# Attention in 256 steps: swaps issued by GpSimd, query pieces a step sooner, outputs ahead of the rests, high parts and value products a step later

## What is computed

```python
q = _rms_norm(x @ wq_a.T, q_norm_w) @ wq_b.T                 # 32 heads of 128 + 64
q_pe = _apply_rope(q_pe, cos, sin)                           # x1*cos - x2*sin, x1*sin + x2*cos
kv_c, k_pe = split(x @ wkv_a.T)                              # 64 latent, 64 rotated
k_nope, v = split(_rms_norm(kv_c, kv_norm_w) @ wkv_b.T)
scores = (q_nope . k_nope + q_pe . k_pe) * scale             # causal
out = softmax(scores) @ v
return out @ wo.T
```

## Time and profile before

| | us |
|---|---|
| median of 3 runs | 1619.09 |
| lowest, highest | 1617.4, 1630.4 |
| the profiled execution's time | 1624.83 |
| its span, first to last instruction | 1622.9 |
| long `least` of the first and of the last step start at | 259.5, 1380.0 |

### The profile page before, as it was taken

The page is one execution under the profiler, slowest core; times in us unless marked ns, Lnnn a source line. Parts: engine busy times, 40 slices in busy tenths (PEclk is TensorE's granted clock), DMA queues, the critical chain, the costliest instruction groups (busy, mean ns, idle before and its releaser), DMA issues. The chain is left out here.

```text
span 1622.9 us, 31480 instructions
## 1 busy us (share of the span) xinstructions
PE 1314.2 (81%) x12688; PEld 965.0 (59%) x12688; DVE 1058.3 (65%) x1441; ACT 940.8 (58%) x1466; POOL 660.6 (41%) x512
## 2 busy tenths in 40 slices
PE   4899976777788787777888777788877788599997
PEld 4678764555555555555555555555555555488886
DVE  3755527777777777777778777677877678422221
ACT  3554426766667676666767766676767677412111
POOL 0211104555555654455556545555655652000000
PEclk8999989999899999999999999999999999799998
DMA  4111035999998999999999999999999999733331
GB/s 148 42 36 52 26 105 110 171 183 181 175 190 171 193 172 183 184 185 187 185 189 185 184 183 186 189 180 187 181 187 187 185 187 185 200 116 119 137 131 65
DMA packets 673150, 253.36 MB, mean 156 GB/s; under 512 B 606336, under 2 KB 650112, under 8 KB 670080
## 3 DMA queue, kind: packets, MB, share of 16 engines
q1 hardware_dynamic: 670304, 242.68, 75.4%
q0 software_dynamic: 2720, 8.92, 1.7%
HBM read 58.60 MB, written 25.17 MB: 52 GB/s over the span
## 5 line engine op out<-in xcount | busy, mean ns | idle before, releaser
L816 DVE TENSOR_TENSOR prob_hl_sb<-prob_sb,prob_hl_sb 128x1152 f16<-128x1152 f32 x256 | 428.1, 1672 | 166.7 <-ACT prob_hl_sb L730 165.9
L667 PE MATMUL acc<-ch,prob_t_sb 128*128 128x65 f16 x2304 | 250.5, 199 | 204.1 <-DMA prob_t_sb<-prob_hl_sb 146.3
L667 PEld LDWEIGHTS acc<-ch,prob_t_sb 128*128 128x128 f16 x2304 | 217.2, 99 | 245.4 <-DMA prob_t_sb<-prob_hl_sb 120.6
L730 ACT ACTIVATE prob_hl_sb<-prob_sb 128x1152 f16<-128x1152 f32 x256 | 297.6, 1163 | 62.1 <-DMA prob_t_sb<-prob_hl_sb 60.8
L811 DVE TENSOR_REDUCE shift_sb<-score_long 128x1 f32<-128x1024 f32 (+3 forms) x256 | 260.5, 1018 | 92.9 <-PE score_long L653 92.9
L722 ACT ACTIVATE prob_sb<-score_long,shift_sb 128x1024 f32<-128x1024 f32 (+3 forms) x256 | 243.2, 950 | 101.6 <-DVE shift_sb L811 99.7
L794 POOL TENSOR_TENSOR rot_sb<-rot_sb,sinT_sb 128x512 f32<-128x512 f32 x62 | 97.8, 1577 | 382.7 <-DMA rot_sb<-qf_sb 382.7
L668 PE MATMUL acc<-cl,prob_t_sb 128*128 128x64 f16 x2304 | 249.8, 196 | 0.0
L669 PE MATMUL acc<-ch,prob_t_sb 128*128 128x65 f16 x2304 | 249.0, 197 | 0.0
L669 PEld LDWEIGHTS acc<-ch,prob_t_sb 128*128 128x128 f16 x2304 | 219.7, 100 | 0.0
L668 PEld LDWEIGHTS acc<-cl,prob_t_sb 128*128 128x128 f16 x2304 | 219.3, 101 | 0.0
(11 more groups left out here) (161 smaller groups left out, 2659.6 us busy)
## 6 DMA issues: line engine op xcount, KB each, us to landing
o_nat_sb<-o SPq DMA_DIRECT2D x18, 1024.0 KB, 5.1
rot_sb<-qf_sb SPq DMA_DIRECT2D x256, 64.0 KB, 2.1
o<-o_sb SPq DMA_DIRECT2D x32, 512.0 KB, 3.9
wqk_sb<-wqk SPq DMA_DIRECT2D x32, 320.0 KB, 3.3
wo_sb<-wo SPq DMA_DIRECT2D x16, 512.0 KB, 4.3
y_in_sb<-y POOLq DMA_DIRECT2D x18, 256.0 KB, 3.0
x_sb<-x SPq DMA_DIRECT2D x4, 1024.0 KB, 4.9
y<-y_sb SPq DMA_DIRECT2D x16, 256.0 KB, 2.0
```

Of the source, the lines that this page charges most:

```text
L667: nc.tensor.matmul(acc[:, at:at + KVL + 1], hi, high, start=(j == 0), stop=False)
L730: nc.scalar.activation(prob_hl[:, s % NHL, 0, :], prob[:, s % 2, :], ACT.Copy).then_inc(hi_ready, 1)
L816: nc.vector.tensor_tensor(prob_hl[:, s % NHL, 1, :], prob[:, s % 2, :], prob_hl[:, s % NHL, 0, :], ALU.subtract).then_inc(lo_ready, 1)
```

## The change

The swaps of all pairs but the first are issued by GpSimd, each ahead of the rests of the chunk before it. Pieces are projected and taken a step sooner, or three steps sooner, and their high parts formed a step later or at the same place. `LAG` goes from 4 to 5, and the buffers of high and low parts from 3 to 4. On ScalarE `high(s-1)` moves behind the long exponential of step s. On VectorE `outputs` stands ahead of `low`. The weights of a later pair come a step sooner.

```diff
-    LAG = 4
+    LAG = 5
-    NHL, NPT = 3, 4
+    NHL, NPT = 4, 4
...
-        PIECE = {0: (1, 2), 1: (1, 3), 4: (2, 0), 5: (2, 1)}
-        HIGH = {0: (0,), 1: (1,), 5: (2,), 6: (3,)}
+        PIECE = {0: (1, 3), 3: (2, 0), 4: (2, 1), 7: (2, 2)}
+        PIECE_FIRST = {0: (1, 2), 1: (1, 3), 4: (2, 0), 5: (2, 1), 7: (2, 2)}
+        HIGH = {1: (0,), 2: (1,), 5: (2,), 6: (3,)}
...
-        ABSORB_AT, WH_AT = 2, 3
+        absorb_at, high_weights_at = lambda s: s % WIN == (2 if s < WIN else 1), lambda s: s % WIN == (3 if s < WIN else 2)
...
-            swap_halves(2)
             for s in range(STEPS):
                 w, u = s // WIN, s % WIN
                 turn(s)
-                if u == 0 and w + 1 < WINS:
-                    swap_halves(2 * (w + 1) + 1)
...
-                if u == 4:
-                    if w + 2 < WINS:
-                        swap_halves(2 * (w + 2))
-                    if w >= 1:
-                        store(w - 1)
+                if u == LAG and w >= 1:
+                    store(w - 1)
...
                 exp(s, LONG)
+                if s >= 1:
+                    high(s - 1)
                 exp(s, SHORT)
...
-                high(s)
+            high(STEPS - 1)
...
+            for k in range(2, 2 * WINS):
+
+                c = k % 2
+                at = slice(c * 512, (c + 1) * 512)
+                swap_halves(k)
+                if k > 2:
+                    query_low(k - 1)
+                pool.wait_ge(rot_in[c], 64 * (k // 2))
                 nc.gpsimd.tensor_tensor(rot[:, c, :], rot[:, c, :], sinT[:, at], ALU.mult)
...
-                if 1 <= s <= STEPS:
-                    low(s - 1)
                 t = s - LAG
                 if t >= 0 and t % 2 == 1:
                     outputs(t)
-                if s < STEPS and u == WH_AT and w + 2 < WINS:
+                if 1 <= s <= STEPS:
+                    low(s - 1)
+                if s < STEPS and high_weights_at(s) and w + 2 < WINS:
                     weights_low(w + 2)
```

More of the change, by code:

```diff
@@ L497, in attention @@
             sem(n) for n in ("proj_mm", "proj_out", "rot_mul", "rot_add", "qh_ready", "ql_ready"))
-        rot_in = [sem("rot_in0"), sem("rot_in1")]
+        first_in, rot_in = [sem("first_in0"), sem("first_in1")], [sem("rot_in0"), sem("rot_in1")]
         first_mul, first_add, first_low, tables_ready = sem("first_mul"), sem("first_add"), sem("first_low"), sem("tables_ready")
@@ L520, in columns @@
             return slice(0, split) if kind == LONG else slice(split, ROW)
-        PIECE = {0: (1, 2), 1: (1, 3), 4: (2, 0), 5: (2, 1)}
-        HIGH = {0: (0,), 1: (1,), 5: (2,), 6: (3,)}
+        PIECE = {0: (1, 3), 3: (2, 0), 4: (2, 1), 7: (2, 2)}
+        PIECE_FIRST = {0: (1, 2), 1: (1, 3), 4: (2, 0), 5: (2, 1), 7: (2, 2)}
+        HIGH = {1: (0,), 2: (1,), 5: (2,), 6: (3,)}
         HIGH_FIRST = {3: (0, 1), 6: (2, 3)}
-        ABSORB_AT, WH_AT = 2, 3
+        absorb_at, high_weights_at = lambda s: s % WIN == (2 if s < WIN else 1), lambda s: s % WIN == (3 if s < WIN else 2)
         def piece_at(s):
-            ahead, place = PIECE.get(s % WIN, (0, 0))
+            ahead, place = (PIECE_FIRST if s < WIN else PIECE).get(s % WIN, (0, 0))
             pair = s // WIN + ahead
@@ L558, in swap_halves @@
                     for to, of in ((base, base + half), (base + half, base)):
-                        sp.dma_start(rot[to:to + half, c, :], qf[of:of + half, c, h, :]).then_inc(rot_in[c], 16)
+                        sp.dma_start(rot[to:to + half, c, :], qf[of:of + half, c, h, :]).then_inc(first_in[c], 16)
             def turn(s):
@@ L707, in _ @@
                         project(n)
-                    if u == ABSORB_AT:
+                    if absorb_at(s):
                         pe.wait_ge(proj_out, min(4 * (w + 2), 4 * WINS))
@@ L780, in _ @@
                                          scale=kvw2[:, 0:1]).then_inc(wo_ready, 1)
-                if u == WH_AT and w + 2 < WINS:
+                if high_weights_at(s) and w + 2 < WINS:
                     weights_high(w + 2)
-                high(s)
+            high(STEPS - 1)
         @block.gpsimd
@@ L788, in _, with swap_halves, query_low @@
             pool.wait_ge(first_low, 2)
-            for k in range(2, 2 * WINS):
+            def swap_halves(k):
+                c = k % 2
+                pool.wait_ge(proj_out, 2 * k + 2)
+                half = ROPE // 2
+                for h, base in ((0, KVL), (1, 0)):
+                    for to, of in ((base, base + half), (base + half, base)):
+                        pool.dma_start(rot[to:to + half, c, :], qf[of:of + half, c, h, :]).then_inc(rot_in[c], 16)
+            def query_low(k):
                 p, c = k // 2, k % 2
                 at = slice(c * 512, (c + 1) * 512)
-                pool.wait_ge(rot_in[c], 64 * (k // 2 + 1))
+                for h in range(2):
+                    pool.wait_ge(qh_ready, 2 * k + h + 1)
+                    nc.gpsimd.tensor_tensor(ql[:, 2 * (p % 2) + h, at], qf[:, c, h, :], qh[:, 2 * (p % 2) + h, at],
+                                            ALU.subtract).then_inc(ql_ready, 1)
+            for k in range(2, 2 * WINS):
+                c = k % 2
+                at = slice(c * 512, (c + 1) * 512)
[3 more added lines that the diff above has]
+                pool.wait_ge(rot_in[c], 64 * (k // 2))
                 nc.gpsimd.tensor_tensor(rot[:, c, :], rot[:, c, :], sinT[:, at], ALU.mult)
@@ L801, in _ @@
                                             ALU.add).then_inc(rot_add, 1)
[L802 to L805, removed]
+            query_low(2 * WINS - 1)
         @block.vector
@@ L851, in _ @@
                 at = slice(c * 512, (c + 1) * 512)
-                dve.wait_ge(rot_in[c], 64)
+                dve.wait_ge(first_in[c], 64)
                 nc.vector.tensor_tensor(rot[:, c, :], rot[:, c, :], sinT[:, at], ALU.mult)
```

## The result

The changed kernel takes 1728.51 us (1726.02 to 1730.85, 4 runs) against 1619.83 us; the ratio is 1.0656, 95% interval 1.0616 to 1.0697. 1725 us was forecast. The profiled execution took 1727.55 us, its span is 1725.6 us.

What follows compares the result with a forecast made beforehand. No engine was full; waiting order bound the kernel at 4.39 us a step. A closed chain of 4.82 us over 255 steps adds 110 us, less 3 at the tail: 1619 to about 1725 us, range 1655 to 1775.

Steps and rivals of the forecast that it cites:

- The chain: VectorE and ScalarE, each step: long `least`, long `exp`, `high`, `low` in closed order; 4.82 us with weights, against 4.39.
- The size of `low`: VectorE's `low`, lengthened where GpSimd computes beside it: mean kept at 1.672 us, bounds 1.35 and 1.90.
- Rival 1: `low` on VectorE runs nearly alone in the chain: 4.50 to 4.58 us a step, 1644 to 1664 us; chance 0.11.
- The prediction's bound: VectorE's `low` beside GpSimd: contention lengthens a `low` by at most one GpSimd instruction; longest seen 2.468 us.
- The stop: Once a window ScalarE waits 4.4 us for GpSimd's rotated query piece; it goes, alone worth up to 136 us.
- Outputs, lag, buffers at nothing: Outputs ahead of `low` on VectorE, lag of five, fourth buffers: costed at nothing, as the wait that follows covers them.
- GpSimd: Moved swaps cost GpSimd 0.54 us per issue, 4.3 a window; with arithmetic 24.2 us, under the window.
- Rival 2: GpSimd falls behind on top of the chain, swap issues taking 1.80 us or more: 1787 us; chance 0.06.
- The waits: VectorE's `low` waits for `high` in nearly every step, 1.4 us each, some 350 us in all against 165.9.
- The tail: After the last `low`, SyncE's backlog of transposes is gone: some 3 us less.
- (3): Faster: the removed stop and lighter SyncE queue count, the chain does not bind; as little as 1483 us; chance 0.05.
- (4): No change: `low` alone nearly everywhere and a shorter tail meet the gain elsewhere, 1619 to 1635 us; chance 0.04.

Runs made afterwards that it cites:

- e1: Changed kernel with `high` back as the last instruction of ScalarE's step; 1523.87 us, ratio 0.9431 to the kernel before.
- e2: Kernel before with only `high(s-1)` moved behind the long exponential of step s; 1795.53 us, ratio 1.1094 to the kernel before.
- e3: Changed kernel with `high(s-1)` one place later, behind the short exponential too; 1799.44 us, one run.
- e5: Changed kernel with GpSimd's rotation working on 32 of the 512 columns of a chunk; 1694.82 us, one run.
- e4: Changed kernel with `outputs` behind `low` again, as in the kernel before; 1802.19 us, one run.
- e6: Kernel before with swaps on GpSimd and the new places of pieces and weights; 1575.36 us, ratio 0.9707 to the kernel before.
- e8: Kernel of e1 with `outputs` behind `low` too; 1524.75 us, ratio 0.9420 to the kernel before.
- e9: Kernel of e1 with the swaps issued by SyncE again, at their old places; 1606.53 us, ratio 0.9912 to the kernel before.
- e10: Kernel of e1 with three buffers of high and low parts, lag 5 kept; 1594.41 us, ratio 0.9818 to the kernel before.

## Why the prediction was right

Point by point, by its own steps.

*The chain.* Its existence is shown by e1 and e2. e3 to e5 show that the time follows its terms, once what each edit does to `low` and to the wait for scores is counted too. Forecast 4.82 us a step, measured 4.80. The terms, forecast and measured: `least` 1.018, 1.015; `exp` 0.950, 0.955; `high` 1.163, 1.153; `low` 1.672, 1.576; `weights_low` 1.136, 1.345 and a gap ahead of it. That the sum is so near is in part luck, as two misses hide each other: `low` was 0.10 us a step too long, which is 24 us in all, and the weights with what hangs on them (TensorE's late scores at `u == 3`, not seen in the prediction) were too short. Chain of the measured terms: 1.015 + 0.04 + 0.855 + 1.153 + 0.03 + 1.496 = 4.59; what is left to 4.80 is 0.21 a step, 1.7 us a window, where 1.06 stood.

*The size of `low`.* That GpSimd's arithmetic lengthens it is shown by e5. The mean of before was a guess that came out near: with the same arithmetic it is 1.41, 1.47, 1.58 and 1.78 us in e3, e4, the changed kernel and e1. Rival 1, `low` nearly alone, did not come, though e3 with 1.41 is close to it. The prediction's bound, that a `low` grows by at most one GpSimd instruction, holds in the changed kernel (the longest took 2.45 us) and not in general: in e1 one took 3.92 us, beside two of GpSimd's rests in a row.

*The stop.* It went, as forecast, and ScalarE's wait with it. As a gain by itself it was sized too large: not up to 136 us but 47 (e6), since ScalarE then waits longer for the transposes, late already in the earlier trace rows. This term did not enter the sum, because the chain covers it.

*Outputs, lag, buffers at nothing.* Right in this kernel, and e4 shows what the cover is worth (74 us). Lag and buffers together give 51 us once the chain is open.

*GpSimd.* A swap's issue took 0.498 us at the median and 0.508 on the mean, forecast 0.54. The changed kernel's row:

```profile
L793 POOL DMA_DIRECT2D rot_sb<-qf_sb x248: 498/498/671, 257.6 to 1421.9; - x124
```

Rival 2 needed 1.80 and has no sign; the longest took 0.671 us. The lock-out of GpSimd's descriptors, of which the Trainium skill tells (DMA: Bandwidth & Descriptors, SWDGE vs HWDGE vs iDMA), left no mark on the issues here. The landing took longer, 4.2 us at the median against 2.1 before; why is not shown. GpSimd waits 1.5 us in all for it in the changed kernel, as the rests cover it, but 110.5 us in e1.

*The waits.* 350 us forecast for `low`, 354.7 measured.

*The tail.* I had 3 us less; it is 242.5 against 242.9 us from the last `least` to the end. This step failed, for little.

The rivals (3) and (4) on the other side were given 0.09. e1 shows how near they were: the stop's removal and the buffers are a gain of 5.7%, and one line turns it into a loss of 6.6%.

## What to carry to other kernels

When an instruction is moved behind one that waits for another engine, write down the closed path through both rows of instructions: with one pass per step and no slack, the sum of its terms is a lower bound of the step, however idle the engines are. Work inside that wait is free, and the same work outside it is paid (the outputs: nothing in e8 with the chain open, 74 us in e4 with it closed). The terms do not stay as they are when the chain shifts: with the chain closed `low` went from 1.41 to 1.58 us on the mean over these runs. And where a change bundles several parts, the loss can be one line's: here all parts but the moved `high` give the fastest kernel of this study, 1524 us (e8, with outputs moved back too, takes the same).

## What the runs showed of the hardware

- TensorE's granted clock fell with the chain: 0.906 of full speed on the mean (0.942 before), although the stops of 4.4 us are gone. Behind an idle stretch of 2.98 us, ahead of the projection above, its matmuls run at the lower level, 1.2 GHz: the granted clock is 0.50 of full speed from 851 to 857 us, and 1.00 again at 858. As the next scores are on the path for that once, this adds to the 0.34 us wait, by how much was not measured; the long `least` waits for scores 11.2 us in all, so it costs little.
- With two engines bound to each other the steps repeat almost exactly, and a single `low` of a window meets the same GpSimd instruction each time: in the changed kernel the lows of five places of a window take 1.36 us at the median, the other three 2.17, 2.04 and 1.67, while in e1 seven of the eight places have lows from under 1.4 to over 2.1. That makes the mean of `low` a matter of phase, not of GpSimd's load: it is busy 509 of 800 us beside the changed kernel's lows of 1.58 us and 654 of 800 beside e1's of 1.78, but only 439 in the kernel before with 1.67.
- The issue of one transpose by SyncE is no fixed cost: median 2.85 us in the kernel before, 3.26 in the changed kernel, 3.49 in e1. How much is moved does not explain it: the changed kernel moves less, 171 GB/s against 184, and e9 and e10, with 188 and 187, have 2.93 and 3.39. The longer issues are in the kernels whose swaps GpSimd issues, so that they can run beside transposes; the cause itself was not tested.
